# A GRU and a routed expert layer on one core: recurrent weights first, a smaller projected head, and the copy of x in sixteen pieces beside the steps

## What is computed

```python
# x: 16 sequences of 256 tokens, 512 wide; cond_2048: the GRU's first state
def cell(h, x):
    gi = x @ W_ih + b_ih
    gh = h @ W_hh + b_hh
    i_r, i_z, i_n = jnp.split(gi, 3, axis=-1)
    h_r, h_z, h_n = jnp.split(gh, 3, axis=-1)
    r = jax.nn.sigmoid(i_r + h_r)
    z = jax.nn.sigmoid(i_z + h_z)
    n = jnp.tanh(i_n + r * h_n)
    h_new = (1.0 - z) * n + z * h
    return (h_new, h_new)
hs = scan(cell, cond_2048, x over its 256 tokens)
# routed layer on hs: 8 experts, 352 hidden, the best two of each token
scores = hs @ Wg.T
w = softmax of the best two scores, 0 elsewhere
y = sum over e of w[e] * ((silu(hs @ W1[e].T) * (hs @ W2[e].T)) @ W3[e].T)
out = x + y
```

## Time and profile before

| | us |
|---|---|
| median of the timed runs | 1712.79 (1710.22 to 1712.98) |
| the profiled execution, its own time | 1723.49 |
| its span | 1721.8 |
| PE busy | 1459.1 (85%) |
| DVE busy | 1126.6 (65%) |
| ACT busy | 673.1 (39%) |
| POOL busy | 404.7 (24%) |
| HBM read, written | 217.47 MB, 55.79 MB |

### The profile page before, as it was taken

How to read it: one execution, slowest core, us unless ns; L and a number is a source line. 1 busy time by engine, 2 the same in 40 slices (tenths; PEclk the granted TensorE clock), 3 DMA queues, 4 the chain that set the end, 5 groups by cost and what they waited for, 6 DMA issues and landing times.

```text
span 1721.8 us, 69764 instructions
## 1 busy us (share of the span) xinstructions
PE 1459.1 (85%) x29785; PEld 1171.3 (68%) x29785; DVE 1126.6 (65%) x4419; ACT 673.1 (39%) x1564; POOL 404.7 (24%) x857
## 2 busy tenths in 40 slices
PE   4778675699999999999999999999999888766766
PEld 4666565677777777777777777777778676534433
DVE  5587676777777777777777777777777777612221
ACT  5354453333433343334333433343334333323333
POOL 1001221122222222222222222222222222232223
PEclk9788887699999999999999999999999988878888
DMA  8756464434444444444444444444444444557764
GB/s 273 230 167 179 122 156 124 170 119 128 159 137 137 137 162 137 137 137 142 127 125 138 150 139 133 124 136 137 137 137 137 137 137 137 165 190 239 226 216 151
DMA packets 93734, 265.71 MB, mean 154 GB/s; under 512 B 33007, under 2 KB 50415, under 8 KB 83312
## 3 DMA queue, kind: packets, MB, share of 16 engines
q1 hardware_dynamic: 75472, 227.60, 40.3%
q0 software_dynamic: 17952, 33.64, 8.7%
HBM read 217.47 MB, written 55.79 MB: 159 GB/s over the span
## 4 chain that ended last, share of the span: by engine, by line
PE 52%; DVE 24%; issue 7%; DMA 6%; ACT 5%; another core or an unknown queue 2%; POOL 2%; SPq 1%; DVEq 0%; POOLq 0%; ACTq 0%
PE gr_ps L1052 10%; PE gn_bank L1052 9%; PE b_ps L1073 8%; PE gz_ps L1052 6%; PE y_ps L1136 5%; PE b_ps L1099 4%; DVE hn L850 4%; DVE zpre L850 4%; PE gi_ps L1073 3%; PE a_ps L1099 3%; DMA work<-h_tok,mt 3%; DMA mt<-meta 3%; DVE hlog L882 2%; ACT zs L677 2%
## 5 line engine op out<-in xcount | busy, mean ns | idle before, releaser
L1052 PE MATMUL gr_ps<-hlog,whh 128*128 128x32 f16 x8192 | 249.7, 178 | 158.1 <-DVE hlog L885 137.5
L1052 PEld LDWEIGHTS gr_ps<-hlog,whh 128*128 128x128 f16 x8192 | 226.0, 96 | 230.3 <-DVE hlog L885 191.2
L1052 PE MATMUL gz_ps<-hlog,whh 128*128 128x32 f16 x8192 | 248.7, 178 | 6.1 <-issue 5.9
L1052 PE MATMUL gn_bank<-hlog,whh 128*128 128x32 f16 x8192 | 247.2, 177 | 6.0 <-issue 5.8
L535 POOL DMA_INDIRECT out_y<-work,mt x71 | 114.7, 1616 | 579.4 <-ACT work L721 400.5
L1052 PEld LDWEIGHTS gz_ps<-hlog,whh 128*128 128x128 f16 x8192 | 226.4, 97 | 7.6 <-issue 7.6
L1052 PEld LDWEIGHTS gn_bank<-hlog,whh 128*128 128x128 f16 x8192 | 225.5, 96 | 6.9 <-issue 6.7
L1073 PE MATMUL b_ps<-x_split,wih 128*128 128x512 f32 (+1 forms) x792 | 198.7, 396 | 0.3
L1136 PE MATMUL y_ps<-wbuf,work 128*128 128x512 f16 x639 | 176.7, 413 | 1.8 <-ACT work L698 1.8
L1099 PE MATMUL a_ps<-wbuf,work 128*128 128x352 f16 x852 | 151.2, 331 | 23.8 <-issue 23.8
L675 ACT ACTIVATE nt<-npre 128x64 f32<-128x64 f32 x256 | 65.7, 257 | 258.9 <-DVE npre L869 239.5
(11 more groups left out here) (159 smaller groups left out, 2135.5 us busy)
## 6 DMA issues: line engine op xcount, KB each, us to landing
wbuf<-wscr SPq DMA_DIRECT2D x71, 1410.0 KB
wbuf<-wscr SPq DMA_DIRECT2D x71, 768.0 KB
h_tok<-xrow SPq DMA_DIRECT2D x32, 256.0 KB
x_raw<-in_x_feat SPq DMA_DIRECT2D x7, 1024.0 KB, 6.1
wscr<-wbuf SPq DMA_DIRECT2D x9, 768.0 KB, 4.5
wscr<-wbuf SPq DMA_DIRECT2D x9, 706.0 KB, 4.2
wscr<-wbuf SPq DMA_DIRECT2D x9, 704.0 KB, 4.7
work<-in_w_units SPq DMA_DIRECT2D x8, 512.0 KB
```

Source lines behind the costliest of these rows:

```text
L1052: mm = pe.matmul(dst[:, j], whh[:, i, k, m * P:(m + 1) * P], h[:, k], start=(k == 0 and i == 0), stop=(k == K - 1 and i == 1))
```

## The change

It has four parts.

1. SyncE loads the recurrent weights ahead of the projection's. ScalarE takes their four magnitudes first, VectorE computes the scale and the high half before it splits the projection's weights, and the low half is made in four instructions, two before part 2 of the projection's weights and two before part 3. ScalarE evicts pieces between its casts.
2. The first chunk is cut at 128 and 256 tokens. The head projects 128 tokens only, tokens 128 to 255 are projected in steps 0 to 5 (two pieces a step, needed from step 8), tokens 256 to 511 in steps 6 to 13 (two and one in turn, needed from step 16).
3. The next chunk's pieces begin at step 16 instead of 14, and its splits and the load behind them (`load_x(2)`) move with them.
4. x is copied to `out` in 16 DMAs of 0.5 MB, issued at steps 9, 11, ..., 39.

```diff
-    pieces = [Piece(0, m, 0, HALF, 1) for m in range(M)]
-    pieces += [Piece(0, m, HALF, TOK, 1) for m in range(M)]
+    QUARTER = TOK // 4
+    FIRST_CUTS = (0, QUARTER, HALF, TOK)
+    pieces = [Piece(0, m, lo, hi, 1) for lo, hi in zip(FIRST_CUTS, FIRST_CUTS[1:]) for m in range(M)]
...
-        G_AT[m].append((HEAD + m, 0))
-    FROM_1 = M + 2
+        G_AT[m // 2].append((HEAD + m, 0))
+        G_AT[M // 2 + m * 2 // 3].append((2 * HEAD + m, 0))
+    FROM_1 = M // 2 + 8 + 2
...
+            for k in range(K):
+                sp.dma_start(whh_raw[:, k], w_hh[:, k]).then_inc(whh_loaded[k], 16)
             for p in range(WI):
                 sp.dma_start(wi_raw(p), w_inproj[p]).then_inc(wi_loaded[p], 16)
-            for k in range(K):
-                sp.dma_start(whh_raw[:, k], w_hh[:, k]).then_inc(whh_loaded[k], 16)
...
-            for i in range(4):
-                n = NTOK // 4
-                sp.dma_start(out[i * n:(i + 1) * n], x_tok[i * n:(i + 1) * n]).then_inc(out_ready, 16)
...
+                i, s = divmod(t - COPY_FROM, 2)
+                if 0 <= i < COPIES and s == 0:
+                    n = NTOK // COPIES
+                    sp.dma_start(out[i * n:(i + 1) * n], x_tok[i * n:(i + 1) * n]).then_inc(out_ready, 16)
...
             split_x(0, 0, 0, HALF)
+            for k in range(K):
+                act.wait_ge(whh_loaded[k], 16)
+                if k:
+                    act.wait_ge(whh_mag, k)
+                S.activation(junk[:], whh_raw[:, k], ACT.Abs, accum_out=mags[:, k:k + 1]).then_inc(whh_mag, 1)
             for p in range(WI):
                 act.wait_ge(wi_loaded[p], 16)
                 S.copy(wih[:, p, 0], wi_raw(p)).then_inc(wi_hi, 1)
-            act.wait_ge(setup, N_BIAS)
-            act.wait_ge(consts, 1)
-            for k in range(K):
-                act.wait_ge(whh_loaded[k], 16)
-                S.activation(junk[:], whh_raw[:, k], ACT.Abs, accum_out=mags[:, k:k + 1]).then_inc(whh_mag, 1)
-                for m in range(MW):
-                    take_piece(k * MW + m)
+                if p == 0:
+                    act.wait_ge(setup, N_BIAS)
+                for m in range(MW * p - MW, MW * p if p < WI - 1 else HEAD):
+                    if m >= 0:
+                        take_piece(m)
             split_x(1, 0, HALF, TOK)
...
-                if t == M:
+                if t == FROM_1 - 2:
                     split_x(2, 1, 0, TOK)
...
                 if t == STEPS // 2:
+                    dve.wait_ge(gi_taken, 3 * HEAD)
+                if t == STEPS // 4:
                     dve.wait_ge(gi_taken, 2 * HEAD)
...
             split_x(0, 0, HALF)
-            for p in range(WI):
-                split_wi(p)
             dve.wait_ge(whh_mag, K)
...
             chain(V.tensor_scalar(whh[:, 0], whh_raw[:], scale(SC_W), None, ALU.mult))
-            chain(V.scalar_tensor_tensor(out=whh[:, 1], in0=whh_raw[:], scalar=scale(SC_W), in1=whh[:, 0],
-                                         op0=ALU.mult, op1=ALU.subtract))
+            for p in range(WI):
+                if p >= 2:
+                    for k in (2 * p - 4, 2 * p - 3):
+                        chain(V.scalar_tensor_tensor(out=whh[:, 1, k], in0=whh_raw[:, k], scalar=scale(SC_W),
+                                                     in1=whh[:, 0, k], op0=ALU.mult, op1=ALU.subtract))
+                split_wi(p)
```

More of the change, by code:

```diff
@@ L57, in gru_moe_kernel @@
     PREP_STEP = 5
+    COPY_FROM, COPIES = 9, 16
     def base(j):
@@ L76, in piece_no @@
     def piece_no(c, m):
-        return 2 * M + (c - 1) * M + m
+        return (len(FIRST_CUTS) - 1) * M + (c - 1) * M + m
     for n, piece in enumerate(pieces):
@@ L127, in gru_moe_kernel @@
     ROUTED_BEFORE_A, PIECES_BEFORE_B, BEFORE_PIECE = {}, {}, {}
-    routed, in_bank, tile_b, tile_a = 0, [0, 0], 0, 0
+    routed, in_bank, tile_b, tile_a = 0, [HEAD - 1, HEAD], 0, 0
     A_BEFORE_R = {}
@@ L374, in wi_raw @@
             return raws[p // 2][:, p % 2 * (MW * K * P):(p % 2 + 1) * (MW * K * P)]
-        N_BIAS, N_MAGS, N_SETUP = 2, 22, 37
+        N_BIAS, N_MAGS, N_SETUP = 2, 22, 40
         def count_of(j):
@@ L533, in add_rows @@
                 else:
-                    pool.wait_ge(out_ready, 64)
+                    pool.wait_ge(out_ready, 16 * COPIES)
                 pool.indirect_dma_start(
@@ L1023, in _ @@
                 prep(t)
-                if t == M + 1:
+                if t == FROM_1 - 1:
                     split_x(2, 0, TOK)
@@ L1058, in project @@
                 if half == 0:
-                    pe.wait_ge(x_lo, p.chunk + 2 if p.chunk else 1 + (p.lo > 0))
+                    pe.wait_ge(x_lo, p.chunk + 2 if p.chunk else 1 + (p.lo >= HALF))
                     if n < HEAD:
```

## The result

| | before | after |
|---|---|---|
| timed runs, median, us | 1711.10 (1700.88 to 1713.97, 9 runs) | 1722.17 (1711.99 to 1726.50, 9 runs) |
| ratio after to before | | 1.0054, 95% interval 1.0029 to 1.0080 |
| profiled execution, us | 1723.49 | 1722.91 |
| its span, us | 1721.8 | 1721.2 |
| PE busy, us | 1459.1 | 1477.7 |

The change made the kernel 0.54% slower, 9 us by the ratio (5 to 14). I had forecast 1708.9 us and a range of 1702 to 1719, so the prediction was wrong. The two profiled executions hardly differ in length. That says nothing against the ratio: the one of before lay 12 us above the median of its timed runs, and the loss is in plain view in the first 60 us.

What follows compares the result with a forecast made beforehand. The prediction took the head to be bound by the recurrent weights and steps 3 to 5 by TensorE's stops beside the copies. Terms 0.4+0.3-9.3+2.1+0.6+0.9+0.4+0.7 gave -3.9 us: 1708.9 us timed, range 1702 to 1719.

Steps and rivals of the forecast that it cites:

- the price of a head piece: Head: each of a piece's 12 matmuls of 128 columns takes 0.120 us, as much as one of 256 columns.
- Head: +0.4: Head, up to VectorE's first gate operation: 46.5 us instead of 46.10, so 0.4 us later.
- Rival D: Head and steps: a 128-column matmul costs 0.24 us; +25 us in all, 1738 us; chance 0.06.
- Copy stops, -9.3: Steps 0 to 5: TensorE's stops go with the moved copies, saving all that four periods had over 4.89 us each.
- Rival E: Steps 3 to 5: the stops aren't the copies' doing and stay; +5.4 us, 1718.2 us; chance 0.09.
- Two pieces a step, +2.1: Steps 0 to 5: TensorE's two pieces make the period 5.30 us against 4.89, 0.41 more for each of five steps.
- First expert's load, +0.3: End of step 0: the load, issued at 39.4 us at the earliest, may come late for ScalarE; 0.3 us lost.
- Copies' later cost, +0.7: Later steps: spread copies share a queue with expert loads and stores and may lengthen POOL's stops; 0.7 us lost.
- rival C: Steps 20 and 36: spread copies lengthen POOL's two later stops; upper price 15.7 us, +11.1 in all, 1723.9 us; chance 0.13.
- My sign, both later stops within 1 us of 8: Steps 20 and 36: POOL's stops would stay within 1 us of 8 us if the forecast held.
- Rival B: Head: 128 columns cost half, 0.060 us a matmul, 0.72 a piece; -9.1 us in all, 1703.7 us; chance 0.16.
- Steps 6 to 31, +1.9 in three terms: Late sigmoid behind weight passes (steps 5, 6) +0.6; two-piece steps among 6 to 13 +0.9; half pieces in steps 16 to 31 +0.4.

Runs made afterwards that it cites:

- warm_head128: The changed kernel with 84 extra 256-column matmuls in TensorE's idle time ahead of the head; ratio to before 0.9989.
- warm_cols128: The changed kernel with 58 extra 128-column matmuls filling the same idle stretch ahead of the head; ratio to before 1.0065.
- oc_head256: The changed kernel with its head cut back to 256 tokens, new load order and spread copies kept; ratio to before 0.9952.
- c_copy_only: The kernel before with only the copies of x changed, to 16 of 0.5 MB at steps 9 to 39; ratio to before 0.9958.
- before2: The kernel before run again without an edit, for a second profile; 1674.27 us on another chip.
- warm_filled: The changed kernel with 84 extra 256-column matmuls ahead of the head and nine more in the hole before the tenth piece; ratio to before 1.0000.
- h_only: The kernel before with only the cuts changed: 128-token head, two pieces a step in steps 0 to 5; ratio to before 1.0105.
- oh_oldcopy: The changed kernel with the four 2 MB copies of x back at their old place; ratio to before 1.0104.
- after2: The changed kernel run again without an edit, on another chip; ratio to before 1.0053.
- o_only: The kernel before with only the order of the loads changed, 256-token head and old copies kept; ratio to before 0.9987.

## Why the prediction was wrong

- **The step that failed** is the price of a head piece: "I take 0.120: 128 columns cost what 256 do", and with it "pieces 0 to 2, at the low clock to begin with". 0.114 was measured (0.112 in warm_head128), but only at the high level. I had carried over from the 256-column head that the clock rises after two pieces. Under 128 columns it did not rise: twelve pieces at 0.213, shown by the trace and by warm_head128, warm_cols128 and oc_head256. The term "Head: +0.4" was +11.7 by the first gate operation (57.83 against 46.10). Of the 13 us between the forecast of -3.9 and the measured +9, it is 11.
- **Rival D** had the right size of a head piece (forecast 0.24, measured 0.213) and the wrong reason, a form that costs double everywhere. In the steps its price was not paid, so its 1738 did not come. I had given it 0.06. A rival on the clock was missing: the first two pieces in the earlier trace rows show a cost of 2.56 to 2.90 at the low level for 256 columns, so that "what if it stays there" could have been worked out, 12 x 2.56 = 30.7 us behind 24. That this comes to what was measured is partly luck: 256 columns take 2.70 there, 128 take 2.56.
- **TensorE's start** at 23.8 was right (24.30), and so were the magnitude pass (16.3; 16.5), the product (18.6; 18.94) and VectorE's first wait in kind (3.4; 4.67).
- **Copy stops, -9.3.** Shown by c_copy_only in kind and nearly in size: 19.57 us for four periods, a ratio worth 7.0 us (4.7 to 9.5). Rival E is dead. The stops themselves are 8.2 of the 9.3; slow pieces behind them are the rest.
- **Two pieces a step, +2.1.** The period was 5.13 (66.65-61.52), not 5.30: 1.2 us.
- **First expert's load, +0.3.** ScalarE's first pass (60.92) did not wait for it, since step 0 was late anyway. That cover came from the loss.
- **Copies' later cost, +0.7; rival C.** POOL's stops at steps 12, 20 and 36 in after, and the one at step 36 in before (the others of before are 15.90 and 8.06):

```profile
141.49 0.19 POOL L559 TENSOR_TENSOR fill<-fill,count 128x8 f32<-128x8 f32 x1 [8.23 <-issue]
187.77 0.19 POOL L559 TENSOR_TENSOR fill<-fill,count 128x8 f32<-128x8 f32 x1 [10.03 <-issue]
291.18 0.19 POOL L559 TENSOR_TENSOR fill<-fill,count 128x8 f32<-128x8 f32 x1 [9.90 <-issue]
```

```profile
286.62 0.20 POOL L556 TENSOR_TENSOR fill<-fill,count 128x8 f32<-128x8 f32 x1 [8.65 <-issue]
```

My sign, both later stops within 1 us of 8, failed. And it is the copies: the stop at step 20 is 7.55 to 8.06 us in the five traces with the old copies and 9.28 to 10.56 in the nine with spread ones, the stop at step 36 8.27 to 8.86 and 9.09 to 11.61. Step 24 takes 10.6 to 12.2 us with the old copies and 12.7 to 15.4 with the spread ones, step 39 18.3 to 18.8 and 19.0 to 21.5. By the means that is 2.6 and 1.2 us, 3.8 where my term was 0.7. So rival C's mechanism is there, at a quarter of its price, and not enough to turn the sign: c_copy_only as a whole is faster, and its lead on before2 is 9.6 us at step 8 and 9.8 at step 59, so other steps give that back. C's time of 1723.9 came close, but the loss is in the head: the right number for a wrong reason. The wait for expert weights was 3.57 us at worst instead of 6.32.
- **Rival B** (half the cost) is refuted by 0.114.
- **Steps 6 to 31, +1.9 in three terms.** Not settled by themselves. warm_filled against oc_head256 says that the cuts cost some 10 us outside the head, the changed kernel against it some 6 (17 by the ratios, of which step 0 is 11.2 late), both more than my terms for the pieces of steps 0 to 31 (2.1+0.6+0.9+0.4 = 4.0). Of that, 2.3 us are in steps 0 to 7 (step 8 starts at 98.59 against 85.11). Why the rest is lost is open, and whether the added matmuls themselves have a part in it wasn't tried.

On the clock, the Trainium skill, "TensorE: Matmul & The Clock Gate", Part 1 on the clock gate, says that time spent busy raises it and that the hardware does not count instructions. Here TensorE is busy for 30.70 of 30.70 us and, in warm_cols128, for 43 without the clock rising; the measurement decides, and busy time alone is no promise of the high level.

## What to carry to other kernels

When a change narrows the matmuls of a stretch that starts on an idle TensorE, work out its time at the lower clock to the very end as a case of its own, and give it a serious chance: a duration read behind the rise does not hold for a shape that may not bring the rise. Filling an idle TensorE with wide matmuls, and in a second run with narrow ones, shows whether the clock is the cause. Before loads are rearranged, look at what stands ahead of the waiting pass on its own engine: taking six evictions from ahead of the last pass gave here what a new order of loads was to give. And judge the parts of a change apart, since a good part (the copies, -7 us) and a bad one (the head, +17) came in one diff.

## What the runs showed of the hardware

- Float32r matmuls with a weight load each take 0.213 us at 128 columns (2.56/12) and 0.225 at 256 (2.70/12, before) at the low level, and 0.112 to 0.114 against 0.120 at the high one. Narrowing from 256 to 128 columns gains some 5% at either level.
- 128-column matmuls of this kind held the high level for nine pieces (12 us) in warm_head128 and did not bring it back in 7.0, 30.7 and 43 us. 256-column ones brought it back within one or two pieces. Where 128-column pieces stand between the float16 recurrent matmuls of the steps, the rise came behind the recurrent matmuls of one step in the changed kernel (the first change on record is at 57.6 us) and only behind those of two in h_only (twice), in warm_cols128 and, the first time, in oh_oldcopy.
- The clock fell during or within 2 us behind an idle time of TensorE of 1.07 us (warm_head128), of 1.01 us (warm_cols128, step 1) and of 0.84 us (after2, step 1). It did not fall behind 0.58 us (oc_head256, in the head) and 0.69 us (warm_filled), nor behind 0.90 and 0.99 us ahead of step 1 (after, warm_head128) or the 0.80 us of the undisturbed steps of before, so that the length of an idle time alone doesn't decide it.
- Beside four DRAM-to-DRAM copies of 2 MB TensorE stops for its next instruction for 8 us in the kernel before (1.05, 3.01 and 4.13 us; 1.59, 2.53 and 3.86 in before2), and the same bytes in 16 pieces at other steps don't stop it there. The stops stand at fixed distances in its instruction stream: 127 and 128 matmuls, each with a weight load, lie between them (in before from the sixth matmul of step 3 to the 25th of step 4, and on to the 13th of `gn_bank` in step 5), and the same in o_only; in h_only 127 lie between two. That points to the supply of instructions, not of data; how the copies hold it up no run shows.
- GpSimd's stops for its next instruction behind its indirect DMAs are 7.55 to 8.06 us at step 20 with the old copies, and 9.28 to 10.56 with 16 copies of 0.5 MB spread over steps 9 to 39.
